# TensorE multiplies the identity into an unused PSUM bank while it waits, at ten places of a six-stage kernel

## What the reference computes

```python
x = x + L0_conv(_gn(x))       # depthwise 3x3 convolution, selective scan in 4 directions, gate, output projection
x = x + L1_conv(_gn(x))       # gates, complex recurrence of 16 steps with a 7x7 kernel's spectrum
t = _to_tokens(x)
t = t + L2_attn(_ln_t(t))     # linear attention with softmaxes, 4 heads
t = t + L2_ffn(_ln_t(t))      # router, 2 of 8 experts
t = t + L3_attn(_ln_t(t))     # 4 layers of linear attention without a softmax, 8 heads each
t = t + L3_ffn(_ln_t(t))      # 16 long spectral filters along the tokens, and 3 taps
```

## Time and profile before

| what | value |
|---|---|
| median of 3 runs | 850.33 us (850.28 to 851.41) |
| the profiled execution's own time | 850.71 us |
| its span | 848.9 us |
| granted TensorE clock, mean over the span | 0.930 of full speed |
| TensorE matmul busy | 665.4 us (78%) |
| VectorE busy | 624.4 us (74%) |
| GpSimd busy | 424.1 us (50%) |
| ScalarE busy | 349.7 us (41%) |

### The profile page before, as it was taken

One profiled execution on the slowest core, in us unless ns is written; L12 is line 12 of the kernel. 1 busy time (PEld: TensorE's weight loads), 2 busy tenths in 40 slices (PEclk: granted clock), 3 DMA queues, 4 the chain that ended last, 5 costly groups with the idle time before them and its releaser, 6 DMA issues. The chain is left out here.

```text
span 848.9 us, 7033 instructions
## 1 busy us (share of the span) xinstructions
PE 665.4 (78%) x2460; PEld 352.4 (42%) x2460; DVE 624.4 (74%) x603; ACT 349.7 (41%) x379; POOL 424.1 (50%) x231
## 2 busy tenths in 40 slices
PE   2788788788797877888777777382867599999997
PEld 2442223222222322223222222161434488888886
DVE  6289999999999899999999569647671424443342
ACT  3485365474653736537335035142003223332231
POOL 5039989899899899999977300000231000000000
PEclk9989999999999999999999888798776589999999
DMA  5044444544444445445454160201900000000000
GB/s 161 3 149 149 156 154 142 178 167 153 150 151 145 153 152 185 140 140 182 152 175 169 53 272 0 107 1 48 349 0 0 1 1 1 0 0 0 0 0 25
DMA packets 27226, 88.33 MB, mean 104 GB/s; under 512 B 3636, under 2 KB 4374, under 8 KB 26462
## 3 DMA queue, kind: packets, MB, share of 16 engines
q1 hardware_dynamic: 27200, 88.01, 29.7%
HBM read 86.87 MB, written 1.13 MB: 104 GB/s over the span
## 5 line engine op out<-in xcount | busy, mean ns | idle before, releaser
L576 POOL TENSOR_TENSOR area<-area 128x1024 f32<-128x1024 f32 x127 | 299.4, 2373 | 75.8 <-DVE area L1088 54.9
L1088 DVE TENSOR_TENSOR_SCAN area<-area,ps 128x1024 f32<-128x1024 f32 x128 | 289.4, 2274 | 0.0
L1370 PE MATMUL ps<-area,cst 128*128 128x512 f32 x512 | 256.1, 624 | 1.4 <-POOL area L576 1.1
L755 ACT ACTIVATE area<-area,floors,par_sb 128x1024 f32<-128x1024 f32 x128 | 158.1, 1239 | 177.5 <-DVE area L1088 175.2
L1081 DVE TENSOR_TENSOR ps<-ps,area 128x1024 f32<-128x1024 f32 x128 | 154.2, 1211 | 7.8 <-PE ps L1349 7.2
L1370 PEld LDWEIGHTS ps<-area,cst 128*128 128x128 f32 x512 | 88.5, 191 | 108.1 <-issue 100.6
L1619 PE MATMUL ps<-stack 128*128 128x512 f32 (+3 forms) x768 | 127.8, 326 | 0.4 <-DVE stack L1271 0.4
L1619 PEld LDWEIGHTS ps<-stack 128*128 128x128 f32 x768 | 117.0, 192 | 11.9 <-issue 2.6
L1349 PE MATMUL ps<-stack,sel 32*128 32x512 f32 x256 | 63.7, 495 | 71.4 <-DVE area L1088 67.2
L437 DVE COPY area<-ps 64x1024 f32<-64x1024 f32 x32 | 39.3, 1227 | 85.7 <-PE ps L1619 85.7
L1349 PEld LDWEIGHTS ps<-stack,sel 32*128 32x128 f32 x256 | 23.7, 182 | 162.8 <-DVE area L1088 139.3
(11 more groups left out here) (285 smaller groups left out, 651.0 us busy)
## 6 DMA issues: line engine op xcount, KB each, us to landing
area<-c_rows SPq DMA_DIRECT2D x128, 512.0 KB, 3.8
area<-phi_scaled SPq DMA_DIRECT2D x1, 4104.0 KB, 25.3
area<-in_m_phi_dram SPq DMA_DIRECT2D x4, 1024.0 KB, 8.6
area<-phi_scaled SPq DMA_DIRECT2D x1, 4096.0 KB, 14.9
area<-in_q_t_dram SPq DMA_DIRECT2D x1, 1024.0 KB, 14.1
area<-in_dft_dram SPq DMA_DIRECT2D x1, 784.0 KB
area<-in_m_u_dram SPq DMA_DIRECT2D x1, 768.0 KB, 6.1
area<-in_conv_w_dram SPq DMA_DIRECT2D x1, 576.0 KB, 6.0
```

Source lines behind the costliest of these rows:

```text
L576: pool.tensor_tensor(scan_order(prod[:, u % PRODS, :], k), lines(state[:, u % STATES, :], k), lines(c_sb[:, u % COPIES, :], k), MUL).then_ ...
L755: act.activation(decay[:, u % DECAYS, :], delta[:, n % 2, :], ACT.Exp, bias=floors[:, k, i:i + 1], scale=par_sb[:, k, i:i + 1]).then_inc(s ...
L1088: dve.tensor_tensor_scan(state[:, u % STATES, :], decay[:, u % DECAYS, :], drive_pair(u), 0.0, MUL, ADD).then_inc(sig("scanned"), 1)
L1370: mm = pe.matmul(ps[:, 6 + h, :], con("center"), half(prod[:, u % PRODS, :], h), start=False, stop=(u % (UNITS // 2) == UNITS // 2 - 1), s ...
```

## The change

A helper is added to TensorE's program. It multiplies the identity by the first columns of the constants into a bank that holds nothing then; nobody reads the result, no semaphore is counted, and it waits for nothing. It is called ahead of waits at ten places in the text (the three of the layers run four, four and three times), so TensorE reaches each of these waits later by what the products take. No other engine's program is changed.

```diff
+            def keep_busy(bank, times, cols=HALF):
+
+                for _ in range(times):
+                    pe.matmul(ps[:, bank, 0:cols], ident, cst[:, 0:cols], start=True, stop=True)
+
@@ after L1292, ahead of the wait for the convolution's input
             mm.then_inc(sig("w_dt_done"), 1)
+            keep_busy(5, 24, 256)
@@ after m_summed, ahead of the merge
+            keep_busy(5, 5)
             pe.wait_ge(sig("dve_recurred"), 1)
@@ ahead of the softmax attention's turn
+            keep_busy(4, 5)
             pe.wait_ge(sig("normed"), 1)
@@ ahead of the router's turn
+            keep_busy(0, 13)
             pe.wait_ge(sig("normed"), 3)
@@ ahead of the linear attention
+            keep_busy(3, 7)
             pe.wait_ge(sig("normed"), 4)
@@ in each of its layers
                 mm.then_inc(sig("t_done"), 1)
+                keep_busy(0, 1, 256)
                 pe.wait_ge(sig("t_out"), l + 1)
...
                 mm.then_inc(sig("s_done"), 1)
+                keep_busy(0, 1, 256)
                 pe.wait_ge(sig("is_ready"), l + 1)
...
                     pe.matmul(ps[:, 7, 0:P], is_sb, u_sb, start=True, stop=True).then_inc(sig("g_done"), 1)
+                    keep_busy(0, 1, 256)
@@ ahead of the last block's turn
+            keep_busy(6, 6)
             pe.wait_ge(sig("normed"), 5)
```

## The result

The changed kernel takes 845.81 us (median of 6 runs, 845.04 to 847.59); the kernel before took 850.31 (median of 6, 849.15 to 852.65) beside it. The ratio is 0.9946 (95% interval 0.9929 to 0.9963), 4.6 us faster, a third of what was predicted and just outside the range. The profiled execution took 847.59 us with a span of 845.8, the slowest of the six.

What follows compares the result with a forecast made beforehand. TensorE's clock at half behind idle waits was taken to bound its share of the path; gains of 15.6 us less 1.7 at the head gave 13.9 off, 836.4 us. Range: 2.5 us below the likeliest case's 834, up to 845.5.

Steps and rivals of the forecast that it cites:

- The head's loss: Ahead of the first convolution: the fill outlasts the wait, ends at 21.3 to 22.6 us, and costs 1.7 us.
- the 23 us: Sign at the head: the prediction is wrong if the fill there runs past 23 us.
- I take the clock as held for all but the router: Filled waits at merge, softmax attention, Gram matrix and last block leave 1.6 to 2.0 us idle, keeping full clock.
- Softmax attention: Its start: 3.29 us at half clock halve, 1.65 us, less about 0.5 waiting for ScalarE's copy: 1.15 us gained.
- The criterion behind that step: At the filled waits: idle remainders of 1.6 to 2.4 us judged against 1.68 us that held, 2.38 that did not.
- Last block: Convolve's 4.04 us from 681.07 to 685.11 halve, 2.0 us; counted at three quarters, 1.5 us.
- L1600: Product with the tokens behind the layers: from 3.48 to 2.05 us at full clock, 1.4 us gained.
- Router: Turn and L1553: 1.9 us gained if the clock holds throughout; counted half, 0.95 us.
- The second: Remainders of 1.6 to 2.4 us too long, each wait ends at half clock, only layers gain: 844 us; chance 0.12.
- The third: Transposes do not carry the clock, so router and last block lose their gains: 838.9 us; chance 0.07.
- The fourth: Layers stay at half clock, load too thin even with fills, each passing its wait: 845.5 us; chance 0.10.
- The fifth: Identity products do not lift the clock; the head's fill delays the first convolution 12.3 us: 863 us; chance 0.05.

Runs made afterwards that it cites:

- the kernel with early splits: Changed kernel without the head's fill, first two filter-row splits (toep_high, toep_low) moved into the waits of layers 1 and 2: 839.25 us, ratio 0.9855.

## Why the prediction was wrong

The direction was right, and so was the mechanism in the merge, the Gram matrix and the layers. The sum was not: 13.9 us forecast, 4.6 measured. One term was mis-sized (the head), one criterion was wrong (which remainders hold the clock), and one path was overlooked (VectorE's queue). Step by step:

- **The head's loss (1.7 us, 0.7 to 3.0) was mis-sized: 5.0 us alone, 3.5 to 6.6 by its interval.** The formula for the fill held: 10.3 us at full clock and half of the time to the rise, 12.3 and 13.15 us measured. Wrong was where it started. The prediction took 9.41 us from one execution, in which the small weights had landed at 7.35 and the input was ready at 17.65. In the ten others traced here they landed between 7.47 and 9.87 us, and in both with 24 products L1292 began at 9.0, so the fill began at 11.0 and ended at 24.1 and 23.3, past the 23 us that the prediction had named as a sign of being wrong. The 28.92 us taken as the old end of the convolution were also the latest: L760 started at 29.02 there and at 27.41 to 28.54 us in the five other traces without a head fill. Together 32.1 to 33.0 against about 28.3: 4.2 us, which lies within that interval.
- **"I take the clock as held for all but the router" failed.** Softmax attention: 1.15 us of gain forecast, 1.94 of loss measured, through a fall in L1500 and one among the query transposes that the kernel before did not have. The remainder was the forecast 1.8 us. Both falls are in all six traces with five products ahead of that turn, and in neither of the two with six products and one more among the query transposes.
- **The criterion behind that step was a misreading.** The prediction calls the fall after 2.38 us of idleness the earliest. It is so only behind the scan and outside the layers. Inside the scan the trace of the kernel before has the clock fall 1.2 us into work behind a wait of 1.45 us, and again behind waits of 0.89 and 0.70 us with short work between (windows, columns as in the earlier trace rows, then TensorE's timeline):

```profile
190.18:193.59 3.41, 3.41 (x7) 0.87 (x7) 3.41 (x3) 1.33 (x2) 3.41 (x3) 0.50 0.28 115
272.10:275.51 3.41, 3.41 (x6) 1.28 (x5) 3.41 (x3) 1.54 (x2) 3.41 (x2) 0.50 0.72 244
```

```profile
188.99 0.50 PE L1349 MATMUL ps<-stack,sel 32*128 32x512 f32 x2 [1.45 <-DVE area L1088]
189.42 3.07 PE L1370 MATMUL ps<-area,cst 128*128 128x512 f32 x4
...
269.90 0.50 PE L1349 MATMUL ps<-stack,sel 32*128 32x512 f32 x2 [0.89 <-DVE area L1088]
271.10 2.83 PE L1370 MATMUL ps<-area,cst 128*128 128x512 f32 x4 [0.70 <-POOL area L576]
```

So the 1.68 us that held once were no bound. The length of a wait alone does not decide: 2.0 us ahead of the Gram matrix and 1.8 ahead of the merge held in every trace that has these fills, with dense work behind them, and 1.8 us ahead of the softmax attention's turn, with transposes and a wait of 0.34 us behind it, did not.
- **Last block: 1.5 us forecast, 0.15 measured, and L1600: 1.4 forecast, 0.2 measured.** What the second lost is shown: `toep_low` stands ahead of the sum in VectorE's queue. The prediction followed TensorE's path and not what stood in the queue of the engine that takes its result. The splits' late end also stretched the pause behind the fill to 2.89 us instead of 1.6, and the clock fell in it. Without the splits there 1.66 us were left and the clock held in the one trace that has it; that it always would is not shown.
- **Merge 1.9, Gram matrix 2.0, layers without L1600 6.7:** measured 1.92, 2.39, 6.84. These held. **Router 0.95:** 0.47, the clock fell behind its turn, as foreseen. **Other engines at nothing:** VectorE's busy time is 624.0 us, before 624.4, as foreseen.
- **Rivals.** The second (the remainders too long) was true in part: the clock fell behind three of the five fills ahead of merge and turns, but only the last block's wait ended at half clock, and its remainder was not the one that was priced. The third (transposes do not carry the clock) is not borne out: dense transposes raise it at the head, and with 0.93 us left the softmax attention's turn kept it. The fourth (layers at half) was true nowhere. The fifth's mechanism, products that do not lift the clock, is ruled out by the rise in the head, but its place was the right one.

The forecast terms miss by 3.3 us at the head, 3.1 in the softmax attention, 1.2 at L1600, 1.35 in the last block and 0.5 at the router, with 0.5 on the other side: 8.9 of the 9.3 us. The head's 5.0 us are from the measured ratio, the others from one trace each before and after, so the sum is an estimate.

In place of the 5.0 us the changed kernel's profile has 6.91 up to the merge, 2.94 of them behind L760. From L760 to the second group mean it is 466.6 to 466.8 us in six of the traces here and 468.3 to 469.6 in five. The former have a short first fall of the clock in the scan (3.4 us), the latter one of 6.8 us. Two of the six traces without a head fill are among the five, so it happens without one; but both with 24 products are too. Whether those make it likelier, and what decides in an execution, was not tried.

## What to carry to other kernels

Size work that only holds the clock so that it ends before the real input can come, with the fill starting late, the input early and the clock at half; look at the arrivals of more than one execution. Before a length of idleness is called safe, look through the whole trace for falls behind shorter ones. In this kernel the idle remainder alone did not decide; the work and the next wait behind it went with it. And when a stage gets faster, read the queue of the engine that takes its result: what was written there to fill the old wait is now ahead of it.

## What the runs showed of the hardware

- Clock and load: in the layers 20.96 us busy of 27.31, at half clock, did not bring the full clock back, yet 21.77 of 26.98 held it. Without the fills, layers that begin at full clock lose it in the second, in the kernel before and in the one with only the fills ahead of merge and turns.
- The same remainder can hold or fail: ahead of the last turn 1.66 us were left both in the kernel with early splits and in the one with only the fills ahead of merge and turns. In the first the clock stayed full; in the second it fell 2.9 us after the turn's start, at 678.98, for 3.4 us. So a remainder of this size is no promise. The shortest ones tried ahead of a turn, 0.65 to 0.93 us, held each time, five turns in two kernels.
